# Reordered hand-written engine lists of a fused gated-delta attention and mixture-of-experts kernel

## The reference

```
q, k, v = split(silu(causal_conv1d(xn @ w_qkv)))      # 16 key heads, 32 value heads, 128 wide
q, k = l2norm(q) * 128**-0.5, l2norm(k)
for t in range(256):                                   # per sequence and value head, state S is 128 x 128
    S = S * exp(g_t); S = S + k_t (x) ((v_t - k_t S) * beta_t); o_t = q_t S
attention = (rmsnorm(o) * norm_weight * silu(xn @ w_z)) @ w_out
moe = top-2 of 8 experts (silu(x w1g) * (x w1u)) w2, plus a shared expert of the same form
```

## Time and profile before

| | us |
|---|---|
| median of 3 runs (lowest, highest) | 1083.08 (1082.98, 1084.58) |
| the profiled execution | 1077.03 |
| its span, first to last instruction | 1075.2 |
| TensorE, VectorE, ScalarE, GpSimd busy | 1018.8, 803.7, 634.6, 522.2 |
| mean granted TensorE clock | 0.990 |

### The profile page before, as it was taken

How to read it: one execution, slowest core, us unless ns; L and a number is a source line. 1 busy time by engine, 2 the same in 40 slices (tenths; PEclk the granted TensorE clock), 3 DMA queues, 4 the chain that set the end, 5 groups by cost and what they waited for, 6 DMA issues and landing times.

```text
span 1075.2 us, 22259 instructions
## 1 busy us (share of the span) xinstructions
PE 1018.8 (95%) x8190; PEld 781.0 (73%) x8190; DVE 803.7 (75%) x1469; ACT 634.6 (59%) x1176; POOL 522.2 (49%) x1140
## 2 busy tenths in 40 slices
PE   4999999999999999999999999999999999997997
PEld 4765666677778787878686878777777777685876
DVE  4562422368699898898989898988888888888544
ACT  4441221235576768576777777676767675766642
POOL 4500000387283748374655647383838373755620
PEclk8999999999999999999999999999999999998989
DMA  9952111152405152434242333425151514233121
GB/s 323 391 175 95 45 35 64 59 172 40 109 29 126 45 121 62 104 75 131 39 128 44 123 48 119 75 91 109 59 126 40 127 57 109 65 102 54 29 43 49
DMA packets 183513, 103.16 MB, mean 96 GB/s; under 512 B 155632, under 2 KB 169584, under 8 KB 180080
## 3 DMA queue, kind: packets, MB, share of 16 engines
q1 hardware_dynamic: 181872, 97.55, 33.2%
q0 software_dynamic: 1536, 4.20, 1.2%
HBM read 79.77 MB, written 21.95 MB: 95 GB/s over the span
## 4 chain that ended last, share of the span: by engine, by line
PE 54%; DVE 12%; ACT 7%; issue 4%; POOL 2%; DMA 1%; SPq 0%; DVEq 0%; ACTq 0%
PE rg L1591 8%; PE pj L1422 5%; PE rg L1558 5%; PE rg L1574 5%; PE pj L1424 5%; PE pj L1423 5%; DVE nm L1299 4%; DVE shared_down_or_conv L1262 4%; PE rg L1492 3%; PE rg L1566 3%; ACT vn L1234 3%; PE rg L1575 2%; ACT sqk L1188 2%; PE rg L1537 2%; PE rg L1494 2%
## 5 line engine op out<-in xcount | busy, mean ns | idle before, releaser
L1089 POOL TENSOR_TENSOR rows<-rows,shared_down_or_conv 128x126 f32<-128x126 f32 (+22 forms) x496 | 188.7, 380 | 224.8 <-DMA shared_down_or_conv<-n_scratch 187.1
L1262 DVE SCALAR_TENSOR_TENSOR shared_down_or_conv<-pj,taps,shared_down_or_conv 128x510 f32<-128x510 f32 x372 | 275.5, 744 | 26.7 <-ACT shared_down_or_conv L1140 17.6
L1092 POOL TENSOR_TENSOR rows<-rows 128x126 f32<-128x126 f32 (+22 forms) x496 | 196.5, 396 | 38.9
L1422 PE MATMUL pj<-xhi,whi 128*128 128x512 f32 x376 | 163.9, 436 | 0.9 <-DVE shared_down_or_conv L1262 0.9
L1299 DVE SCALAR_TENSOR_TENSOR nm<-rg,wneg,hidden_or_decays 128x512 f32<-128x512 f32 (+1 forms) x256 | 139.3, 609 | 14.2 <-PE rg L1494 14.1
L1424 PE MATMUL pj<-xhi,wlo 128*128 128x512 f32 x376 | 149.2, 397 | 0.0
L1423 PE MATMUL pj<-xlo,whi 128*128 128x512 f32 x376 | 149.1, 397 | 0.0
L1140 ACT ACTIVATE shared_down_or_conv<-pj,taps 128x512 f32<-128x512 f32 x124 | 85.2, 687 | 99.5 <-PE pj L1424 97.6
L1591 PE MATMUL rg<-wo,gated 128*128 128x256 f32 x512 | 131.6, 391 | 0.3 <-DVE nm L1299 0.3
L1591 PEld LDWEIGHTS rg<-wo,gated 128*128 128x128 f32 x512 | 94.8, 193 | 15.4 <-issue 1.7
L1422 PEld LDWEIGHTS pj<-xhi,whi 128*128 128x128 f32 x376 | 71.0, 189 | 39.6 <-issue 21.8
(11 more groups left out here) (238 smaller groups left out, 1981.1 us busy)
## 6 DMA issues: line engine op xcount, KB each, us to landing
hidden_or_decays<-eg_scratch SPq DMA_DIRECT2D x16, 1536.0 KB, 8.1
wraw<-w_heads SPq DMA_DIRECT2D x16, 776.0 KB, 4.4
w1a<-w_up SPq DMA_DIRECT2D x9, 1024.0 KB, 10.9
shared_down_or_conv<-n_scratch SPq DMA_DIRECT2D x32, 256.0 KB, 4.1
w2a<-w_down SPq DMA_DIRECT2D x8, 512.0 KB, 13.3
wo<-w_out SPq DMA_DIRECT2D x16, 256.0 KB, 2.6
n_scratch<-nm SPq DMA_DIRECT2D x64, 64.0 KB, 2.0
rt_scratch<-shared_down_or_conv SPq DMA_DIRECT2D x32, 128.0 KB, 2.4
```

Of the source, the lines that this page charges most:

```text
L1089: gp.tensor_tensor(tmp, rb[:, 0:r, t:t + 1].to_broadcast([P, r, w]), nb[:, t:t + 1, t + 1:].to_broadcast([P, r, w]), ALU.mult).then_inc(el ...
L1092: gp.tensor_tensor(rb[:, 0:r, t + 1:], rb[:, 0:r, t + 1:], tmp, ALU.add).then_inc(elim, 1)
L1262: v.scalar_tensor_tensor(out=y, in0=it.pbank[item][:, :, 0:S - s], scalar=taps[par][:, piece(j)[0], KS - 1 - s:KS - s], in1=y, op0=ALU.mul ...
L1422: te.matmul(bank, whi[par][w], xhi[:, k, cols], start=(k == 0), stop=False)
```

## The change

Only lists change. The three common lists (iterations 1 to 12) are new. In iteration 0 the tail is reordered: VT0 and VT1 move behind P2 and P3 and O3 goes last on TensorE and ScalarE; VectorE's list stays. In iteration 13 TensorE's list begins with Z0, then SO, in place of SO, Z0. No instruction is added or removed, and no size changes.

```
-            ORDER = ("SO P4 Z0 SQ Z1 K0 K1 OUT0 Z2 P5 Z3 K2 OUT1 OUT2 P6 P7 LA1 K3 LA2 OUT3 OUT4 LB1 OUT5 LB2 P0 OUT6 "
-                     "U1_0 U1_1 N21_0 N21_1 P1 U2_0 P2 P3 U2_1 VT0 OUT7 O0 VT1 O1 O2 O3 VT2 VT3").split()
-            ORDER_A = ("SQ SO P4 E0 Z0 E1 Z1 P5 E2 Z2 W SK S4 LA1 E3 P6 LA2 Z3 S5 LB1 P7 S6 LB2 U1_0 P0 U1_1 S7 P1 S0 P2 "
-                       "U2_0 U2_1 S1 P3 O0 VT0 O1 VT1 S2 O2 O3 VT2 S3 VT3").split()
-            ORDER_V = ("SO D0 D1 SQ P4 K0 D2 OUT0 K1 P5 OUT1 K2 D3 OUT2 K3 P6 OUT3 OUT4 OUT5 P7 OUT6 N21_0 P0 N21_1 P1 "
+            ORDER = ("P4 Z0 SO K0 SQ OUT0 Z1 Z2 Z3 P5 OUT1 K1 P6 P7 K2 LA1 K3 LA2 OUT2 OUT3 OUT4 LB1 P0 LB2 OUT5 P1 "
+                     "U1_0 OUT6 U1_1 N21_0 N21_1 U2_0 VT0 U2_1 P2 P3 VT1 OUT7 VT2 O0 O1 O2 O3 VT3").split()
+            ORDER_A = ("P4 SQ E0 Z0 S4 E1 SO Z1 W Z2 Z3 P5 P6 S5 E2 E3 LA1 SK LA2 P7 LB1 S6 LB2 S7 P0 U1_0 U1_1 U2_0 VT0 "
+                       "P1 S0 P2 U2_1 S1 VT1 P3 VT2 O0 O1 S2 S3 O2 O3 VT3").split()
+            ORDER_V = ("D0 D1 P4 SO D2 SQ D3 K0 OUT0 OUT1 P5 K1 K2 K3 P6 OUT2 OUT3 OUT4 P7 OUT5 OUT6 N21_0 N21_1 P0 P1 "
                        "P2 OUT7 P3 O0 O1 O2 O3").split()
...
                     ("SQ K0 Z0 K1 Z1 LA1 K2 Z2 LA2 K3 Z3 LB1 P4 LB2 P5 U1_0 U1_1 P6 N21_0 N21_1 P7 U2_0 U2_1 P0 O0 P1 O1 "
-                     "VT0 P2 VT1 P3 O2 O3 VT2 VT3").split(),
-                    ("SQ Z0 Z1 LA1 Z2 LA2 Z3 LB1 W P4 LB2 P5 S4 U1_0 U1_1 SK P6 S5 U2_0 U2_1 P7 S6 P0 S7 O0 P1 S0 O1 VT0 "
-                     "P2 S1 VT1 P3 S2 O2 O3 VT2 S3 VT3").split(),
+                     "P2 VT0 P3 VT1 O2 VT2 VT3 O3").split(),
+                    ("SQ Z0 Z1 LA1 Z2 LA2 Z3 LB1 W P4 LB2 P5 S4 U1_0 U1_1 SK P6 S5 U2_0 U2_1 P7 S6 P0 S7 O0 P1 S0 O1 "
+                     "P2 S1 VT0 P3 S2 VT1 O2 VT2 S3 VT3 O3").split(),
...
-                    ("SO Z0 P4 Z1 SQ Z2 K0 OUT0 K1 OUT1 Z3 K2 P5 K3 P6 OUT2 P7 LA1 OUT3 LA2 OUT4 LB1 OUT5 LB2 P0 OUT6 "
+                    ("Z0 SO P4 Z1 SQ Z2 K0 OUT0 K1 OUT1 Z3 K2 P5 K3 P6 OUT2 P7 LA1 OUT3 LA2 OUT4 LB1 OUT5 LB2 P0 OUT6 "
```

## The result

The changed kernel takes 1108.38 us in the median of 4 runs (1105.24 to 1111.25), the kernel before 1083.83 beside it: a ratio of 1.0217, 95% interval 1.0173 to 1.0261. It is slower, as forecast, but by 24.5 us and not by 8.6, far above the range. In a second set of runs the ratio was 1.0182 (1.0146 to 1.0218).

The account below looks back on a forecast made before the run. It took the loop K3, elimination, LA1 to set most periods, TensorE close behind. Terms 1.6 + 7.7 - 0.4 - 0.1 = 8.8 us, carried as 8.6 on 1083.08, gave 1091.7 us; range 1085.5 to 1097.

Parts of the forecast that it names:

- The loop bounds, not TensorE's 95%: Common iterations: K3's scaling, transfer, GpSimd's elimination, transfer, LA1, back to K3 sets most periods, 51.03 us each on average.
- TensorE's shorter list turns into a longer wait: TensorE ahead of LA1: at most 1.4 us freed per iteration, about 1 as likely, becomes waiting for the landing.
- Worth nothing: TensorE's gain in the common iterations saves no time except 0.4 us over ten periods.
- The 4.92 us of the loop stay: From LA1's start to the end of K3's scaling, the time stays 4.92 us, K3 still standing directly behind LA1.
- Eleven times 0.7 for D3: D3's two scans move beside GpSimd's elimination, lengthening its chain 0.7 us in each of eleven turns: 7.7 us.
- The rival in which a pair costs its full length (1.26): Elimination: each scan stops GpSimd for its own 0.6 us, 15 us in all, time 1098; chance 5 in 100.
- Iterations 0 and 1, 1.6 us: ScalarE's later O3 in iteration 0 makes K3's scaling of iteration 1 end 1.6 us late; bounds 1.3 gained, 2.5 lost.
- Iterations 12 and 13, 0.1 us saved: LA1 of iteration 13 is set by TensorE's list: 0.1 us saved, 0.3 at most.
- VectorE costs nothing: VectorE's new list takes 48.9 us from K3 to K3, 2 below the loop, so it adds nothing.
- W earlier, nothing: W waits for Z3 some 8 us ahead of LA1; GpSimd idles 13.66 us afterwards, so no cost.

Follow-up runs that it names:

- Changed, K3 first: Changed kernel with K2 and K3 ahead of LA1 and P7 between LA1 and LA2, on TensorE alone: 0.9994 of the kernel before.
- filler: Changed kernel with five matmuls carrying no information ahead of LA1's wait for the landing, iterations 1 to 12: 1.0115 of the kernel before.
- second profile: The changed kernel itself run once more, nothing altered: 1.0182 of the kernel before.
- ends as before: Changed kernel with the list edits of iterations 0 and 13 undone, common lists new: 1.0170 of the kernel before.
- before, D2 late: Kernel before with D2 behind OUT1 on VectorE, outside the elimination, and E2 behind S4 on ScalarE: 1.0229 of the kernel before.
- with D3 back as well: Changed kernel with five filling matmuls ahead of LA1's wait and D3 moved behind P5 on VectorE: 1.0053 of the kernel before.

## Why the prediction was wrong in its size

- *The loop bounds, not TensorE's 95%.* Right. "Changed, K3 first" shows it best: loosening LA1 to K3 alone brings back the whole loss, with the work and VectorE's and ScalarE's lists left as they were.
- *TensorE's shorter list turns into a longer wait.* Right: 22.9 us of waits over eleven turns, 2.1 us per turn.
- *"Worth nothing", and "The 4.92 us of the loop stay".* This is the step that failed. I took idle time of an engine that isn't the bound as free. Behind seven of the waits the granted clock was 0.50, and the first work behind the wait, LA1 and K3, lies on the loop: 4.94 us became 5.8 in the mean, 9.4 us in eleven turns (9.3 of them in the six turns with a low clock), and TensorE, slow for 3 to 10 us more, came last at the next LA1 twice. The filler removes this part (63.8 to 54.1) and 12.7 us of the turns in all. In the sum the term stood at nothing, because rows 5 showed 1.00, where the waits ahead of LA1 are 1.76 us at most. But the trace of the kernel before has longer ones outside the common iterations. In iteration 14 TensorE stands idle for 5.1 us ahead of LA1, and the granted clock behind it is 0.50:

```profile
986.36:991.47 5.11, 0.00 (x0) 0.76 0.86 131
991.48:995.80 4.32, 4.32 (x70) 0.50 0.81 113
```

  That a longer wait can cost the clock could have been read there.
- *Eleven times 0.7 for D3.* 7.1 us measured, 6.7 in the second profile, 6.6 when D3 alone moved. The rival in which a pair costs its full length (1.26) is not what the chains show, though its exclusion is (see the last section).
- *Iterations 0 and 1, 1.6 us.* VectorE's wait for O3 came as worked out, and TensorE's SO waits for the same square, which the prediction left out:

```profile
320.76 0.69 ACT L1244 ACTIVATE sq<-rg 128x512 f32<-128x512 f32 x1
...
321.49 0.75 DVE L1364 SCALAR_TENSOR_TENSOR gated<-rg,nwneg,zs 128x512 f32<-128x512 f32 x1 [2.33 <-ACT sq L1244]
...
321.50 1.07 PE L1582 MATMUL rg<-sq,ones 128*32 128x512 f32 x8 [1.48 <-ACT sq L1244]
```

  K3 of iteration 1 ends 62.3 us behind LA1 of iteration 0, against 61.0 before: 1.3 us, 2.1 in the second profile. The 1.6 is the right size by a tail that cost more (2.4 to 3.1, "ends as before") and a head that gave 1.1 back.
- *Iterations 12 and 13, 0.1 us saved.* Wrong: 2.5 us lost, 1.7 in the second profile. The clock was low behind LA1 of 12 in both; the same failed step. With the filler, which has the same lists, the clock stayed high there and the stretch is 53.3 us, 0.1 over before.
- *VectorE costs nothing.* Nearly right in the changed kernel (4.92 where the clock was high and TensorE waited), but the slack was small: VectorE was late by 0.4 to 0.7 us in three turns of the two profiles in which TensorE didn't wait, and with K3 ahead of LA1 it was VectorE's list that bounded.
- *W earlier, nothing.* No run moved W alone, and no row shows a cost. GpSimd's 3.5 us instruction behind W is what the scans ran into in the experiments, also where W stood as before ("before, D2 late").

## What to carry to other kernels

Follow each dependence that closes on itself an iteration later before believing a busy share, and add up its parts from the timelines: here four sums show for every run, the misses too, in which part the time went, and "chain to LA1" shows whether the loop still bounds. Idle time of TensorE is not free when the first work behind it lies on such a loop: look up the granted clock in windows behind all such waits of the program, and fill the wait or put other work behind it. When an item is moved, look at what it newly stands beside on the engine that shares a port, and at whose bank it now takes.

## What the runs showed of the hardware that was not expected

- In the two profiles of the changed kernel the granted clock fell to 0.50 (1.2 GHz) behind 13 waits of 1.6 to 4.1 us ahead of LA1, for 3.4 to 10 us, but not behind every one: 2.65 us in iteration 7 and 2.13 in the second profile left it at 1.00, as did 2.78 and 2.81 in "ends as before" and all waits up to 1.76 in the common iterations of before. The length of this one wait does not decide it alone: in "changed, K3 first" the clock fell in an iteration with 0.18 us at LA1 and 1.14 us at K3 ahead of it, and in "before, D2 late" behind waits of about 1.7 us at K3. With five matmuls in the wait it never fell in the common iterations (once with D3 back as well). 26 us more of TensorE work made the changed kernel 7 to 11 us faster.
- Beside a chain of 62 small GpSimd instructions each scan costs about 0.3 us: the chain takes 27.1 us with no scan (one chain, rows 6), and in the mean over the eleven turns of all thirteen profiles 28.4 with four, 29.0 with six, 29.6 with eight. The 0.46 that rows 6 give from six to eight is not borne out. Against one long GpSimd instruction a scan stands still until that ends (2.57 us for a scan of 0.66).
- The Trainium skill (SBUF — State Buffer, Who interferes with whom) calls the shared port an exclusive lock for a whole instruction. The long instruction agrees, and so do the small ones. Of 1169 GpSimd instructions of the chains that started while a scan ran, in thirteen profiles, none ended before the scan did; they ended 0.01 to 0.25 us behind it. A scan that started inside a small GpSimd instruction nearly always ended 0.54 to 0.63 us behind that one's end. The price per scan is still less than the 0.66 us of a scan; my reading, which no run tests, is that a part of the blocked instruction's own time passes while it is blocked.
